# Layer 0 of a graph kernel: second PSUM banks for odd quads, deeper rings, one TensorE signal per quad

## What is computed

```python
qk = x @ Wqk + bqk
v = x @ Wv + bv
scores = jnp.sum(qk[dst] * qk[src], axis=-1) / jnp.sqrt(jnp.float32(D))
scores = jnp.clip(scores, -5.0, 5.0)
m = jax.ops.segment_max(scores, dst, num_segments=N)
e = jnp.exp(scores - m[dst])
s = jax.ops.segment_sum(e, dst, num_segments=N)
attn = e / s[dst]
out = jax.ops.segment_sum(attn[:, None] * v[src], dst, num_segments=N)
h = out @ Wo + bo + x            # then LayerNorm, the residual and a second LayerNorm
```

## Time and profile before

| | us |
|---|---|
| three runs | 2995.08, 2976.26, 2990.29 |
| median | 2990.29 |
| profiled execution | 2994.84 |
| its span, first to last instruction | 2993.0 |
| mean granted TensorE clock | 0.826 |

### The profile page before, as it was taken

How to read it: one execution, slowest core, us unless ns; L and a number is a source line. 1 busy time by engine, 2 the same in 40 slices (tenths; PEclk the granted TensorE clock), 3 DMA queues, 4 the chain that set the end, 5 groups by cost and what they waited for, 6 DMA issues and landing times. The chain is left out here.

```text
span 2993.0 us, 52671 instructions
## 1 busy us (share of the span) xinstructions
PE 2201.2 (74%) x14461; PEld 1756.5 (59%) x14461; DVE 1718.3 (57%) x7092; ACT 1126.6 (38%) x2973; POOL 1725.0 (58%) x1739
## 2 busy tenths in 40 slices
PE   7766665666666666667578888887888887888779
PEld 5665665665555666556355555555555665656556
DVE  2355555555555555557346656666666666666766
ACT  2355555555555555555333222222222222222123
POOL 3356666666666666655565656666666666666322
PEclk9687788788788877887788888987888888888879
DMA  5344444444444444432644444444444444444201
GB/s 136 97 117 111 109 112 105 113 113 109 109 111 114 106 112 112 123 88 59 171 148 141 147 142 126 144 143 140 144 146 147 144 131 139 146 146 147 62 20 36
DMA packets 378501, 356.41 MB, mean 119 GB/s; under 512 B 61695, under 2 KB 335743, under 8 KB 371424
## 3 DMA queue, kind: packets, MB, share of 16 engines
q1 hardware_dynamic: 314640, 236.51, 28.3%
q0 software_dynamic: 53248, 109.16, 14.2%
q10 hardware_dynamic: 10320, 7.37, 0.9%
HBM read 338.98 MB, written 13.82 MB: 118 GB/s over the span
## 5 line engine op out<-in xcount | busy, mean ns | idle before, releaser
L846 POOL DMA_INDIRECT rows<-xl_tab,src_cols x832 | 844.0, 1014 | 505.9 <-issue 228.1
L279 POOL DMA_INDIRECT rows<-in_x,src_cols x832 | 796.6, 957 | 537.0 <-issue 208.9
L330 PE MATMUL tile_sums<-gather,rows 128*128 128x128 f32 x1664 | 420.1, 342 | 254.4 <-DVE node_sums L560 172.4
L560 DVE TENSOR_TENSOR node_sums<-node_sums,tile_sums 128x256 f32 x832 | 350.0, 421 | 387.1 <-PE tile_sums L332 182.9
L330 PEld LDWEIGHTS tile_sums<-gather,rows 128*128 128x128 f32 x1664 | 322.9, 241 | 296.7 <-issue 190.1
L320 PE MATMUL p_dst<-window,spread 128*128 128x129 f32 x1664 | 331.1, 333 | 200.9 <-issue 154.1
L1022 DVE SCALAR_TENSOR_TENSOR node_sums<-node_sums,shrunk,tile_sums 128x128 f32 x832 | 280.7, 337 | 238.2 <-remote 175.6
L320 PEld LDWEIGHTS p_dst<-window,spread 128*128 128x128 f32 x1664 | 283.6, 241 | 219.8 <-issue 207.6
L332 PE MATMUL tile_sums<-gather,ones 128*128 128x128 f32 x1664 | 389.8, 323 | 0.0
L548 DVE CUSTOM_DVE_ANT_0 product<-rows,p_dst 128x128 f32<-128x128 f32 x832 | 258.2, 348 | 226.3 <-remote 147.7
L909 PEld LDWEIGHTS z_ps<-spread,window 128*128 128x128 f32 x1664 | 254.6, 221 | 155.2 <-issue 132.9
(11 more groups left out here) (187 smaller groups left out, 2525.7 us busy)
## 6 DMA issues: line engine op xcount, KB each, us to landing
window<-p_tab SPq DMA_DIRECT2D x832, 64.5 KB
attr<-in_attrT SPq DMA_DIRECT2D x52, 1024.0 KB
window<-xr_tab SPq DMA_DIRECT2D x832, 64.0 KB
rel_bc<-rel_rows SPq DMA_DIRECT2D x208, 128.0 KB
rel_bc<-rel_rows SPq DMA_DIRECT2D x52, 512.0 KB
rows<-in_x,src_cols POOLq DMA_INDIRECT x832
rows<-xl_tab,src_cols POOLq DMA_INDIRECT x832
p_tab<-p_rows ACTq DMA_DIRECT2D x13, 258.0 KB, 3.5
```

What stands on the lines that cost most here:

```text
L279: nc.gpsimd.indirect_dma_start(out=rows[:, r, i, :], out_offset=None, in_=t["x"], in_offset=bass.IndirectOffsetOnAxis(ap=src_cols[:, tile: ...
L330: nc.tensor.matmul(tile_sums[k][:, i, 0, :], rows[:, Q % AHEAD0, 2 * k + i, :], gather1[:, Q % 2, 2 * k + i, :], start=True, stop=True)
L560: nc.vector.tensor_tensor(span, span, tile_sums[i // 2][:, i % 2, :, :], ALU.add).then_inc(added, 1)
L846: nc.gpsimd.indirect_dma_start(out=rows[:, r, i, :], out_offset=None, in_=xl_tab, in_offset=bass.IndirectOffsetOnAxis(ap=src_cols[:, tile: ...
```

## The change

For odd quads from 15 to 195 (`PAIRED`), spread_p and score use the banks o_ps and t_ps in place of p_dst, and add_up and add_tile use lr_ps in place of tile_sums. So PE waits for the scores and additions of quad Q-2 (`same_banks`) for all quads from 16 to 196; outside this range for Q-1 as before. The rings get deeper: rows 4 to 8 quads, windows and rel_bc 4 to 6, spread and gather1 2 to 4. The four signals p_spread and summed of a quad are replaced by one, `stepped`, at the last matmul of a step (before make_p); `fetched(Q)` and `added_up(Q)` say what value it has when quad Q was spread or summed. DVE's two waits for halves of a score become one for the quad, and so do those of its additions. The first use of lr_ps by quad 15 waits for the last copy of make_p, and the first of the dense blocks for the additions.

```diff
-    AHEAD0 = 4
+    AHEAD0 = 8
+    RING0 = 4
+    SLOTS0 = 6
     SLOTS = 4
+    PAIRED = range(15, 196, 2)
...
+    def same_banks(Q):
+        return Q - (2 if Q in PAIRED or Q - 1 in PAIRED else 1)
+    def fetched(Q):
+        return Q + 1
+    def added_up(Q):
+        return Q + 3
...
-        window = sb("window", [P, SLOTS, QT, P + 1])
-        rel_bc = sb("rel_bc", [P, SLOTS, QW], BF16)
-        spread = sb("spread", [P, 2, QW])
+        window = sb("window", [P, SLOTS0, QT, P + 1])
+        rel_bc = sb("rel_bc", [P, SLOTS0, QW], BF16)
+        spread = sb("spread", [P, RING0, QW])
...
+        p_dst2 = [bank[:].rearrange("p (k i) d -> p k (i d)", k=2) for bank in (o_ps, t_ps)]
+        tile_sums2 = [bank[:].rearrange("p i (s d) -> p i s d", s=2) for bank in lr_ps]
...
                 for Q in range(quads):
-                    if Q >= SLOTS:
-                        sp.wait_ge(p_spread, 2 * (Q - SLOTS + 1))
+                    if Q >= SLOTS0:
+                        sp.wait_ge(stepped, fetched(Q - SLOTS0))
...
                     if Q >= AHEAD0:
-                        pool.wait_ge(summed, 2 * (Q - AHEAD0 + 1))
+                        pool.wait_ge(stepped, added_up(Q - AHEAD0))
...
                 def spread_p(Q, k):
...
-                    if Q:
-                        pe.wait_ge(scored, 2 * (Q - 1) + k + 1)
+                    if Q and Q != PAIRED[0]:
+                        pe.wait_ge(scored, 2 * same_banks(Q) + k + 1)
+                    bank = p_dst2[k] if Q in PAIRED else p_dst[k]
...
-                    mm.then_inc(p_spread, 1)
+                    return mm
 
                 def add_up(Q, k):
                     if k == 0:
                         pe.wait_ge(onehot_made, Q + 1)
-                    if Q:
-                        pe.wait_ge(added, (Q - 1) * QT + 2 * k + 2)
+                    if Q == PAIRED[0]:
+                        pe.wait_ge(p_kept, 2 * node_groups)
+                    elif Q:
+                        pe.wait_ge(added, same_banks(Q) * QT + 2 * k + 2)
+                    bank = tile_sums2[k] if Q in PAIRED else tile_sums[k]
...
-                    mm.then_inc(summed, 1)
+                    return mm
...
-                spread_p(0, 1)
+                spread_p(0, 1).then_inc(stepped, 1)
                 for T in range(steps):
                     for k in range(2):
                         if T + 1 < quads:
-                            spread_p(T + 1, k)
+                            mm = spread_p(T + 1, k)
                         if 0 <= T - 1 < quads:
-                            add_up(T - 1, k)
+                            mm = add_up(T - 1, k)
+                    if T <= quads:
+                        mm.then_inc(stepped, 1)
...
                     if b == 0:
...
-                        pe.wait_ge(p_kept, 2 * node_groups)
+                        pe.wait_ge(added, tiles_before(0))
...
                     act.wait_ge(apart_made, Q + 1)
-                    if Q >= 2:
-                        act.wait_ge(summed, 2 * (Q - 1))
+                    if Q >= RING0:
+                        act.wait_ge(stepped, added_up(Q - RING0))
...
                 def make_spread(Q):
...
-                    if Q >= 2:
-                        dve.wait_ge(p_spread, 2 * (Q - 1))
+                    if Q >= RING0:
+                        dve.wait_ge(stepped, fetched(Q - RING0))
...
                 def score(Q, k):
-                    dve.wait_ge(p_spread, 2 * Q + k + 1)
                     if k == 0:
+                        dve.wait_ge(stepped, fetched(Q))
...
+                    bank = p_dst2[k] if Q in PAIRED else p_dst[k]
...
                 def add_tile(Q, i, base):
...
-                    if i % 2 == 0:
-                        dve.wait_ge(summed, 2 * Q + i // 2 + 1)
+                    if i == 0:
+                        dve.wait_ge(stepped, added_up(Q))
```

## The result

| | us |
|---|---|
| before, median of 20 runs | 2994.78 |
| after, median of 20 runs | 3003.64 |
| ratio after to before | 1.0036, 95% interval 1.0021 to 1.0050 |
| profiled span, before and after | 2993.0 and 3008.4 |

The change makes the kernel slower by 0.36%, about 11 us (the medians differ by 8.9), where 82 us less were forecast. First the main loop of layer 0. The fences show, of the kernel after, the same stretch of busy times as the earlier trace rows, POOL's group as in the earlier trace rows, and the longest waits as in the earlier trace rows.

A forecast was written before the change was run, and what follows sets the result against it. No engine was full; waiting in rings with late PE signals set 6.0 us a quad. A two-quad ring was to give 5.55, saving 82 us over 182 quads: 2994.8 - 82 - 4.5 = 2908 us, range 2805 to 3045.

The forecast's parts named there:

- POOL is nearest: four cost 4 x 1.26 = 5.0 us.: Layer 0 main loop: a gather takes 956 ns plus 0.30 us, so POOL needs 5.0 of 6.0 us a quad.
- What makes them late no row shows; I take lateness as a measured quantity.: Layer 0 loop: PE's signals reach other engines up to 5 to 7 us after their matmul's row, cause unknown.
- x: Extra lateness of the one combined PE signal in the two-quad ring, taken as 2.4 us, bounds 0 and 3.1.
- (8.7 + x)/2: Time of a paired quad: DVE, ACT, PE and hand-overs 8.7 us for two quads, plus lateness; 5.55 us.
- The banks and the one signal: Paired quads: waits move to Q-2, one signal a step; ring of DVE 3.1, ACT 2.15, PE 3.24 us and signal.
- The turn between scores and spread: Every quad's DVE score, PE spread, signal, DVE score sequence, which the second banks were to take away; no separate size.
- I cost the rings at nothing by themselves.: Deeper rings of rows, windows, spread and one-hots: 0 us alone; DMA share 0.45 was to cover bunched transfers.
- The 26 quads that aren't paired: Layer 0 quads that still wait for Q-1 with the late combined signal: -29 to +22 us for 17, taken as 0.
- The port rule: DVE's tensor_scalar shuts GpSimd out of shared ports: POOL's floor would be 5.5 us a quad; trace showed at most 0.1.
- No change: Rival: lateness stays at 3.1 us with PE's 2.4 GHz stretches, or later signals return each gain; 2972 us, chance 0.18.
- POOL-bound: Rival: lateness under 1.3 us, gathers run back to back at 5.0 us a quad; 2813 us, chance 0.20.
- Slower: Rival: late combined signal holds all engines, PE at 1.2 GHz; 3099 or 3036 us, decides from 12 us ring; chance 0.22.

The follow-up runs named there:

- third call: Third set of follow-up runs, on a fast chip (kernel before: 2547 us): the whole changed kernel against the kernel before, 2526.0 us, ratio 0.9933.

## Why the prediction was wrong

**"POOL is nearest: four cost 4 x 1.26 = 5.0 us."** This is the step that failed. It takes the busy time and the 0.30 us behind it for the whole cost of a gather, and puts what follows a streak at nothing for POOL. On a fast chip that is right (5.05 us a quad with rows of half the bytes, 4.95 for the changed kernel); on the chip of the prediction a gather costs 1.50 us, so POOL's floor was 6.0, where the kernel stood. Nothing on PE, DVE or ACT could gain. The rows that could have told were there: 351.6 us of idle by 639 gathers is 0.55 a gather, 0.25 above the 0.30, and the pause behind eight gathers has twice the excess of that behind four (1.87 and 1.02 us). I read that as waiting in a ring. The section of the Trainium skill that the prediction cites (Perfetto Trace Analysis, Per-engine timelines) has a part for gathers that I passed over: the reported end is when the last descriptor has been written, and what comes behind it lies outside. The trace agrees as far as it goes, since in the loop of the kernel after the bytes of a gather have moved about 1.5 us behind the end of its row; which step behind that end takes the 0.25 us no run here shows.

**"What makes them late no row shows; I take lateness as a measured quantity."** The quantity was measured rightly and used wrongly. x was set at 2.4 us, 2.6 with the hand-overs of 0.2; the signal took 2.7 in the cycle above and 2.2 in the median of the 80 (2.0 to 4.3). But it isn't a term beside others. The signal comes 1.8 to 2.1 us behind the end of a streak of eight, wherever PE's last sum ended before, so x is what is left of the gathers' time when the engines' ring is done: a shorter ring should make a longer x. By that the sum (8.7 + x)/2 could not go under 6.0. Rows of the pattern stood in the earlier trace rows: the longest wait of POOL ended about 2 us behind the end of a streak of gathers. I tied the lateness to the clock level instead, since 1.2 GHz came with a prompt signal. With half the gathers the clock is at 1.00 from 240 to 700 us and the ring falls to 3.4 us a quad.

**The banks and the one signal.** The mechanism is as told: once for two quads DVE waits, before the scores, and the ring has its four links. Their sizes in the cycle above: DVE 3.0 (3.1 taken), ACT 2.2 (2.15), PE 4.1 (3.24, by the mean clock of 0.81; from 712.5 to 716.6 us the granted clock is 0.58), the signal 2.7 (2.6 with hand-overs). Sum 12.0 for 11.1, and nearly all of the difference is PE's. It would be wrong to call PE's term the cause: the same program, with the same ring, takes 4.95 us a quad on the fast chip of the third call. The turn between scores and spread was worth nothing, by the second banks alone (0.9992).

**"I cost the rings at nothing by themselves."** Wrong by 0.6% on a slow chip (1.0060 by the ring of eight alone): it lets 32 gathers run in one streak at the start, and make_p's signals and SP's issues come late beside it, 24 us at the first clip. On a fast chip it is likely what gives the 0.7%, which was not tested alone. The cover that I named, the DMA share of 0.45, was the wrong resource: leaving out three of four window transfers gave 11 us.

**The 26 quads that aren't paired** were taken at 0; clips of quads 192 to 207 take 102.0 us against 106.3, so -4.

**The port rule** (the Trainium skill, SBUF — State Buffer, Who interferes with whom) wanted 0.5 us a quad for DVE's tensor_scalar beside gathers. On a fast chip gathers follow each other each 1.26 us through whole quads with their make_spread, so nothing of it is seen, as the earlier trace rows said.

**The rivals.** "No change" came nearest, in time (2972, 32 us too low) and in its second reason, that each gain is given back by a later signal; its first, that lateness belongs to PE's stretches at 2.4 GHz, is wrong. "POOL-bound" is the right mechanism with 1.26 in place of 1.50, and so put 190 us too low (2813). "Slower" told a clock falling (0.81 to 0.78 in the loop, it did) and a ring at 12 us, the point from which it decides; that the ring stopped there because the gathers hold it there is my reading of the streaks, and the combined signal with a ring of four costs nothing (0.9999, 0.9982, 0.9965). That the time did go up by 0.36% is the ring of eight's doing, which no rival had. What would make the forecast wrong was named last, "POOL's streaks of gathers", and not costed.

## What to carry to other kernels

Divide the time of a loop by the count of each engine's instructions, gathers first, before taking the idle time beside them for waiting on others. Sort an engine's pauses by the length of the streak that they follow: pauses that grow with it (1.32 us behind four, 2.17 behind eight here) are a price of the instructions themselves. When signals of one engine reach all others late, look at what runs until just before they arrive, not only at the engine that sends them. Run a deeper ring for the bound engine alone, and look at the start of the loop, where others must get through beside its first streak: here it undid what its companions gave on a slow chip.

## What the runs showed of the hardware

- In layer 0 a gather instruction (128 indices, 512 bytes each) cost 1.48 to 1.50 us in a long run in four of the six sets of runs (each on the chip it got) and at most 1.26 us in two, with the same 0.96 us row; in layer 1 it was 1.64 and 1.34 on one chip of each kind. On a slow chip the cost doesn't depend on bytes (256 or 512) or rows (64 or 128). Why chips differ, and where the 0.25 us are spent, is open.
- Beside gathers given each 1.26 us on a slow chip, TensorE's signals and SP's issues are late. The wait that they end goes by the streak: POOL pauses for 1.32 us behind four gathers, 2.17 behind eight. Held signals arrive 3 to 5 us behind a streak of 32, up to 25.5 us after their matmul; four window DMAs take 12.6 us to issue in place of 2. The bytes of 31 of the 32 gathers had moved by 46 us, when the streak ends.
- Given each 1.48 us, they hold nothing that the start shows (0.04 us).
